# Two fused attention functions: query-first scores issued two slots ahead, and the maxima turned in a step's last slot or inside a projection

## The reference, cut to what matters

```
x = x + _L0_attn_ref(_layernorm(x), ...)    # softmax attention with rotary q, k, and a gated linear-attention recall
x = x + _L0_xattn_ref(ctx_512, ...)         # learned graph, top-k mask
x = x + _L0_ffn_ref(_layernorm(x), ...)     # mixture of experts, 8 choices per token
x = x + _L1_attn_ref(_layernorm(x), ...)    # softmax(q k^T / sqrt(32)) v, then w_o
x = x + _L1_xattn_ref(_layernorm(x), ctx_512, ...)   # the same with keys and values from ctx, causal
x = x + _L1_ffn_ref(_layernorm(x), ...)     # gated network with a Walsh-Hadamard transform
```

## Time and profile before

| what | value |
|---|---|
| measured, median of 3 runs | 3028.73 us |
| the profiled execution: its span | 3028.2 us |
| what lies around the span, by the median | 0.5 us |
| PE busy | 2476.7 us, 82% of the span |
| PEld (weight loads) | 1644.7 us, 54% |
| DVE busy | 1884.0 us, 62% |
| ACT busy | 1239.5 us, 41% |
| POOL busy | 851.9 us, 28% |

### The profile page before, as it was taken

The page is one execution under the profiler, slowest core; times in us unless marked ns, Lnnn a source line. Parts: engine busy times, 40 slices in busy tenths (PEclk is TensorE's granted clock), DMA queues, the critical chain, the costliest instruction groups (busy, mean ns, idle before and its releaser), DMA issues. The chain is left out here.

```text
span 3028.2 us, 35090 instructions
## 1 busy us (share of the span) xinstructions
PE 2476.7 (82%) x12822; PEld 1644.7 (54%) x12822; DVE 1884.0 (62%) x2959; ACT 1239.5 (41%) x1873; POOL 851.9 (28%) x1176
## 2 busy tenths in 40 slices
PE   5898989864443357999448999999999879999999
PEld 4454545321222237998334554545555538888887
DVE  3766575627899985778557777565655444444443
ACT  2444444428656625666103433334333323333332
POOL 2232222215657634555343332001211110000000
PEclk8999999976665678999768999999999979999999
DMA  3213132212222346988585655334433423101000
GB/s 117 65 43 84 43 84 46 70 61 77 77 80 77 108 163 213 308 300 289 158 185 136 159 146 157 88 89 104 109 95 91 115 80 127 42 0 42 1 28 15
DMA packets 186940, 323.55 MB, mean 107 GB/s; under 512 B 20450, under 2 KB 52066, under 8 KB 186788
## 3 DMA queue, kind: packets, MB, share of 16 engines
q1 hardware_dynamic: 168356, 270.44, 30.0%
q0 software_dynamic: 15360, 50.34, 6.3%
q10 hardware_dynamic: 3072, 0.79, 0.1%
HBM read 182.30 MB, written 62.92 MB: 81 GB/s over the span
## 5 line engine op out<-in xcount | busy, mean ns | idle before, releaser
L757 DVE TENSOR_REDUCE at_negmax<-at_ps 128x2 f32<-128x1024 f32 (+3 forms) x256 | 259.1, 1016 | 120.3 <-PE at_ps L523 63.1
L670 ACT ACTIVATE at_probs<-at_ps 128x1024 f32<-128x1024 f32 (+3 forms) x256 | 221.7, 866 | 267.4 <-PE at_ps L538 263.3
L1367 DVE TENSOR_REDUCE a_negmax<-a_ps 128x2 f32<-128x1024 f32 x128 | 155.2, 1217 | 136.4 <-PE a_ps L1120 135.8
L59 PE MATMUL ff_ps<-ff_xnT_hi,ff_s_hi 128*128 128x512 f32 x512 | 200.8, 392 | 5.1 <-DVE ff_xnT_lo L2878 5.1
L60 PE MATMUL ff_ps<-ff_xnT_lo,ff_s_hi 128*128 128x512 f32 x512 | 200.1, 391 | 0.0
L61 PE MATMUL ff_ps<-ff_xnT_hi,ff_s_lo 128*128 128x512 f32 x512 | 200.1, 391 | 0.0
L1946 ACT ACTIVATE gr_act_signs<-gr_signed,gr_test 128x512 bf16<-128x512 f32 x248 | 177.4, 717 | 42.3 <-POOL gr_test L2339 20.4
L2908 DVE TENSOR_TENSOR ff_hid<-ff_hid,ff_ps 128x512 f32<-128x512 f32 x64 | 44.0, 688 | 238.6 <-ACT ff_hid L2853 238.6
L538 PE MATMUL at_ps<-at_qk 98*128 98x512 f32 (+3 forms) x512 | 171.7, 417 | 21.0 <-DMA at_qk<-at_mrow 10.6
L1268 ACT ACTIVATE a_probs<-a_ps 128x1024 f32<-128x1024 f32 x128 | 130.8, 1023 | 135.2 <-PE a_ps L1138 134.6
L518 PE MATMUL at_ps<-at_qk 96*128 96x512 f32 (+3 forms) x512 | 162.9, 382 | 19.0 <-DVE at_xnT_lo L818 8.9
(11 more groups left out here) (431 smaller groups left out, 6640.1 us busy)
## 6 DMA issues: line engine op xcount, KB each, us to landing
at_qk<-at_part SPq DMA_DIRECT2D x384, 128.0 KB
first_gu<-in_L_ffn_w_gate_up_dram SPq DMA_DIRECT2D x32, 1024.0 KB, 13.4
a_qk<-a_part SPq DMA_DIRECT2D x192, 128.0 KB
first_d<-in_L_ffn_w_down_dram SPq DMA_DIRECT2D x32, 512.0 KB, 13.6
out_rows<-ex_y SPq DMA_DIRECT2D x32, 512.0 KB
gr_aside_raw<-in_L_ffn_W_dram SPq DMA_DIRECT2D x48, 256.0 KB, 3.1
w13T<-gr_aside_out SPq DMA_DIRECT2D x32, 256.0 KB, 3.2
shared_x<-x_after_cross SPq DMA_DIRECT2D x8, 1024.0 KB
```

Source lines behind the costliest of these rows:

```text
L59: pe.matmul(out, lh, rh, start=start, stop=False, skip_group_check=True)
L670: act.activation(probs[:, t % 2, 2 * w:2 * w + 2, lo:S], banks(("kq", g, s), lo), ACT.Exp, scale=SCALE).then_inc(free(("kq", g, s)), 1)
L757: dve.reduce_max(negmax[:, g % 2, :].rearrange("p (j t) -> p j t", t=NT)[:, 2 * w:2 * w + 2, t], banks(("qk", g, s), 0, width(g, t)), AX.X ...
L1367: dve.reduce_max(negmax[:, g % 2, :].rearrange("p (j t) -> p j t", t=NT)[:, 2 * w:2 * w + 2, t], banks(("qk", g, s)), AX.X, negate=True).t ...
```

## The change

**Second function.** `score_units(g, s)` puts the query-first unit two slots ahead (LEAD = 2) of its old place: step g issues unit (g+1, s+2) in slot s up to slot 5, and units 0 and 1 of group g+2 in slots 6 and 7. Step -1 does three units in slot 0 to get ahead. The maxima of g+1 are turned in slot 7 (MAXIMA_AT), behind that slot's scores, and the rows are copied and sent there, by the engines' programs too, and no longer at the step's end.

**First function.** In an even step g above 0 the units are two ahead and end with slot 5; slots 6 and 7 have none, and the maxima are turned in slot 7. Step 0 has no lead. In an odd step slots 0 to 5 hold unit s of g+1 as before, slot 6 holds units 6 and 7, and slot 7 units 0 and 1 of g+2. The maxima are then turned inside the first projection, after two of its four contraction chunks for q. The outputs move from the end of step 4k and slots 1, 3, 5 of step 4k+1 to slots 1, 3, 5, 7 of step 4k+1. Weighting and sums stay one half per slot.

The diff, without the repeats of the same edits in ACT's and DVE's programs of the first function:

```diff
@@ -353,6 +353,13 @@
         def reciprocal_part(s):
             return s - 2 if 2 <= s < 2 + NT else None
 
+        LEAD, MAXIMA_AT = 2, PAIRS - 1
+
+        def score_units(g, s):
+            at = PAIRS * (g + 1) + s + LEAD
+            units = range(LEAD + 1) if (g, s) == (-1, 0) else (at,) if g >= -1 else ()
+            return [(n // PAIRS, n % PAIRS) for n in units if has(n // PAIRS)]
+
         SUMS_AT = {1: 0, 6: 1, "mid_end": 2, "end": 3}
 
         def sums_at(g, when):
@@ -365,8 +372,10 @@
             for s in range(PAIRS):
                 if has(g):
                     place("kq", g, s)
-                if has(g + 1):
-                    place("qk", g + 1, s)
+                for unit_of in score_units(g, s):
+                    place("qk", *unit_of)
+                if s == MAXIMA_AT and has(g + 1):
+                    place("mx", g + 1)
                 kind, b, u = unit(g, s)
                 if kind == "o" or kind == "v":
                     place(kind, b, u)
@@ -377,8 +386,6 @@
                     place("xT", b, 1)
                 if weight(g, s) is not None:
                     place("w", weight(g, s))
-            if has(g + 1):
-                place("mx", g + 1)
             if has(g + 3):
                 place("p", g + 3)
 
@@ -637,8 +644,10 @@
                 for s in range(PAIRS):
                     if has(g):
                         scores_kq(g, s)
-                    if has(g + 1):
-                        scores_qk(g + 1, s)
+                    for unit_of in score_units(g, s):
+                        scores_qk(*unit_of)
+                    if s == MAXIMA_AT and has(g + 1):
+                        turn_maxima(g + 1)
                     if s >= 2 and has(g):
                         half(g, s - 2)
                     if s < 2 and has(g - 1):
@@ -654,8 +663,6 @@
                         turn_x(b)
                     if weight(g, s) is not None:
                         turn_weight(weight(g, s))
-                if has(g + 1):
-                    turn_maxima(g + 1)
                 if has(g + 3):
                     project(g + 3)
 
@@ -716,8 +723,8 @@
                             act.copy(xnT[0][:, 2 * i:2 * i + 2, :], banks(("xT", b, i))).then_inc(xT_hi, 1)
                     if weight(g, s) is not None:
                         keep_weight(weight(g, s))
-                if has(g + 1):
-                    maxima_rows(g + 1)
+                    if s == MAXIMA_AT and has(g + 1):
+                        maxima_rows(g + 1)
                 if has(g + 3):
                     if g + 3 >= 1:
                         act.wait_ge(stack_in[(g + 2) % STACKS], 16 * 3 * QUAD * ((g + 2) // STACKS + 1))
@@ -789,8 +796,10 @@
                     dve.wait_ge(masks_made, 2)
                     dve.tensor_copy(above_r, above).then_inc(mask_ready, 1)
                 for s in range(PAIRS):
-                    if has(g + 1):
-                        maxima(g + 1, s)
+                    for unit_of in score_units(g, s):
+                        maxima(*unit_of)
+                    if s == MAXIMA_AT and has(g + 1):
+                        maxima_rows(g + 1)
                     if reciprocal_part(s) is not None and has(g - 1):
                         reciprocals(g - 1, reciprocal_part(s))
                     for b, j in sums_at(g, s):
@@ -955,7 +962,8 @@
         ps = ctx.enter_context(nc.psum_tensor(f"{tag}_ps", [P, 8, 512], F32))
         NUM, SUMS = 6, 7
         STEPS = range(1 - NC, G + 2)
-        OUT_AT = {(0, PAIRS): 0, (1, 1): 1, (1, 3): 2, (1, 5): 3}
+        OUT_AT = {(1, 1): 0, (1, 3): 1, (1, 5): 2, (1, 7): 3}
+        LEAD, MAXIMA_AT = 2, PAIRS - 1
         VALUES_AT = {(2, 0): 0, (2, PAIRS): 1}
 
         def has(g):
@@ -963,6 +971,18 @@
 
         def chunk(g):
             return CHUNKS[g % NC]
+
+        def score_units(g, s):
+            if g % 2 == 0:
+                ahead = LEAD if g > 0 else 0
+                units = [(g + 1, s + ahead)] if s + ahead < PAIRS else []
+            elif s < PAIRS - LEAD or g < 0:
+                units = [(g + 1, s)]
+            elif s == PAIRS - LEAD:
+                units = [(g + 1, s + n) for n in range(LEAD)]
+            else:
+                units = [(g + 2, n) for n in range(LEAD)]
+            return [u for u in units if has(u[0])]
 
         def out_unit(g, s):
             t, b = OUT_AT.get((g % NC, s)), g // NC - 1
@@ -1006,8 +1026,10 @@
             for s in range(PAIRS):
                 if has(g):
                     place("kq", g, s)
-                if has(g + 1):
-                    place("qk", g + 1, s)
+                for unit_of in score_units(g, s):
+                    place("qk", *unit_of)
+                if g % 2 == 0 and s == MAXIMA_AT and has(g + 1):
+                    place("mx", g + 1)
                 if linear_unit(g, s, 2) is not None:
                     place("m", linear_unit(g, s, 2))
                 if linear_unit(g, s, 4) is not None:
@@ -1019,7 +1041,7 @@
                 if turn_unit(g, s) is not None:
                     place("xT", turn_unit(g, s), 0)
                     place("xT", turn_unit(g, s), 1)
-            if has(g + 1):
+            if g % 2 and has(g + 1):
                 place("mx", g + 1)
             if g % 2 and has(g + 3):
                 place("p", g + 3)
@@ -1190,12 +1212,14 @@
                     mm = pe.matmul(bank(key, i), spare(m)[:, 1, i * P:(i + 1) * P], features(m)[:, 0, :], start=True, stop=True, skip_group_check=True)
                 mm.then_inc(l_ready, 1)
 
-            def project(g):
+            def project(g, between=None):
                 at = chunk(g) * P
                 wait_drained(pe, "xT", g // NC, 1)
                 key = claim("p", g)
                 for i, w in enumerate((wqT, wkT)):
                     for dc in range(NC):
+                        if between is not None and (i, dc) == (0, 2):
+                            turn_maxima(between)
                         mm = split_mm(pe, bank(key, i), [p[:, dc, at:at + P] for p in w], [p[:, dc, :] for p in xnT], dc == 0, dc == NC - 1)
                 mm.then_inc(p_ready, 1)
 
@@ -1248,11 +1274,11 @@
                         values(*values_unit(g, s))
                     if turn_unit(g, s) is not None:
                         turn_x(turn_unit(g, s))
-                if has(g + 1):
+                if g % 2 and has(g + 3):
+                    project(g + 3, g + 1 if has(g + 1) else None)
+                    project(g + 4)
+                elif g % 2 and has(g + 1):
                     turn_maxima(g + 1)
-                if g % 2 and has(g + 3):
-                    project(g + 3)
-                    project(g + 4)
                 if out_unit(g, PAIRS):
                     outputs(*out_unit(g, PAIRS))
                 if values_unit(g, PAIRS):
...
```

## The result

The median is 3052.39 us (3048.65 to 3054.88, 4 runs) against 3030.36 for the kernel before in the same measurement: ratio 1.0065, 95% interval 1.0047 to 1.0082, so 14 to 25 us slower. The forecast was 3032, its range ended at 3046. The profiled execution took 3050.13 us with a span of 3048.3, 20.1 over the earlier trace rows.

A forecast was written before the change was run, and what follows sets the result against it. PE's waits were taken to bound the kernel. First function +13.0 us, second -8.5, sum +4.5 on the profiled execution gave 3033.2; 1.2 off for the clock terms gave 3032 us, range 3012 to 3046.

The forecast's parts named there:

- The sum of the second function: Second function: -23.4 us for waits that go, +14.9 us for waits that come, together -8.5 us.
- the late stack: Second function, slot 6 of steps 4 and 8: PE waits 5.0 and 3.8 us for the stack; +14.2 us with clock.
- the low clock: PE runs at granted clock 0.50 after a long wait: 2.7 us added to each wait of over 3 us.
- the removed transposes: Second function, maxima turned at the step's end: 23 waits of PE for the last reduction go, -18.6 us.
- just in time: Second function, step 0: the queue is done with the stack before slot 6 needs it, so no wait was charged.
- covered: Second function, steps with c = 1, 2 and 3: outputs or values before slot 6 cover the stack, no wait charged.
- with the clock at 0.50 behind it: First function, near 310 and 455 us: low clock follows the projection's wait; 5.7 us each with it, +11.4 us.
- What is late next is nothing: Second function, step's end: once the reduction wait goes, no other wait replaces it; the projection hides the rows' copying.
- The knot of outputs, oT, the copy of the recall and the projection's bank: First function, steps 5 and 9: later outputs make PE wait 3.0 to 3.5 us before the projection; +11.4 us with clock.
- the rows of maxima and the stack at step 5: First function, after steps 4, 8, 12: PE idles 3.4 us for rows, then 2.6 for the stack; +5.4 us in all.
- the stack that decides everywhere: Slower rival, chance 0.18: stacks pace steps from their start; landing 1.2 us later costs 12 us in ten causal steps, 3044.
- The term for the DMA of the last rows: Second function, last boundary but one: rows' DMA starts 1.3 us earlier among queued loads; -2 us, bounds 0 to -7.5.

The follow-up runs named there:

- second_only: Only the second attention function has the change, the first is that of the kernel before: 3044.25 us, ratio 1.0037 to before.
- second_load_behind: As second_only, but SyncE issues the 1 MB load of x of steps 0, 4 and 8 behind the stack: 3028.27 us, ratio 0.9990 to before.
- its control: The kernel before with only the load of x issued behind the stack: 3035.98 us beside 3035.11, ratio 0.9995.
- first_only: Only the first attention function has the change, the second is that of the kernel before: 3041.70 us, ratio 1.0037 to before.
- first_outs_early: As first_only, but the four output tiles lie in slots 0, 1, 3, 5 instead of 1, 3, 5, 7: 3035.89 us, ratio 1.0021 to before.

## Why the prediction was wrong

- **The second function's sign: the failed step.** The sum of the second function, -23.4 + 14.9, failed in three of its terms, which the next points take one by one: the late stack was put too low, the low clock was charged only to waits of over 3 us, and the removed transposes were credited in full. Its terms regrouped by the steps above (forecast, measured in the profile; the forecasts come to -8.9, 0.4 off the prediction's own sum by rounding): steps 0, 4, 8: +11.8, +20.1; the steps with g mod 4 = 1: -0.5, +6.2; steps 16, 20, 24: -3.1, +2.5; the other sixteen: -11.7, -9.4; 29 and 30: -4.2, -5.1; the start -1.2, -1.6. So 22 us lie between forecast and measurement, 8 in the late stacks and 12 in steps where PE still waits about as long as before and mostly at a lower clock.
- **The late stack: right cause, too small.** Steps 4 and 8 were forecast with waits of 5.0 and 3.8 us; they are 6.9 and 6.3. I read the end of the transfers from the first microsecond in which the queue's share fell. The queue went on with a few packets (8 in the microsecond from 1744; 17 and 1 in the two from 1865), and the pair waits for the last. Step 0, "just in time", waited 3.16 us (1.26 in second_only), and step 1, "covered", 1.84: a margin of nothing, read from one execution, is no zero. second_load_behind and its control show that the 1 MB ahead in the queue is a cause, worth 14 us once the stack is due early. It is not all of the wait: 3.15 and 3.92 us stayed without it.
- **The clock behind short waits: missed.** I charged the low clock only to waits of over 3 us, because these were the rows that I had looked at. In the profile after, steps 5, 9, 13, 16, 21 and 24 lost 1.5 to 1.7 us of PE time each to it, behind waits of 0.2 to 1.3 us in pairs. Part of this is the luck of one execution: by the counts above the old order loses the clock in 3 of the seven steps with g mod 4 = 1 on average and the new one in 4.3, which at 1.5 us each is an estimate of 2 us and not 6.
- **The clock behind the projection's stall.** At the 2.84 us stalls of the profile after, where I did charge it, it didn't come: 5.4 us too much in the first function, so the sign "with the clock at 0.50 behind it" failed in this execution, and it came behind one of the two in first_only. The 5.4 us were made up by stack waits of 1.95, 0.54 and 1.58 us in steps 3, 7 and 11 (forecast: about 0.5 each, of which 0.2 net) and by the low clock of steps 5 and 9.
- **The transposes: 13 of the 18.6 us.** Seven of those 23 still wait, 0.5 to 1.6 us, 5.5 in sum: three for the bank of a weight that DVE or ScalarE is still splitting, four for a reduction on a DVE that lags, in steps 12, 16, 20 and 24. "What is late next is nothing" was wrong for them. (The six steps with g mod 4 = 1 that the 18.6 leaves out waited 4.0 us in sum in the trace of before, not 4.2.)
- **The first function: right by its steps.** The knot of outputs, oT, the copy of the recall and the projection's bank stalled PE for 2.84 us twice, forecast 3.0 to 3.5, and the rows of maxima and the stack at step 5 took 3.29 and 2.20 us, forecast 3.4 and 2.6 (the 3.4 doesn't follow from its own terms, 3.9 less 1.0; the sum doesn't use it). That the total, 12.4, came so near to 13.0 is in part luck: the errors named under the projection's stall cancel.
- **The rival that came closest** was the stack that decides everywhere, by its size (3044 with a range to 3046), but not by its mechanism: the causal steps 20 and 24 waited 0.55 and 0.43 us, much as in the forecast (0.5 and 0.2), and no other causal step did.
- **The term for the DMA of the last rows** was -2 for step 29. The wait went from 7.48 to 6.70 us, -0.8, and lay between 4.4 and 8.9 in the experiments. The rule of the Trainium skill (DMA: Bandwidth & Descriptors, "Queues, rings and completion order") would have made it about -5; this pair of traces does not bear that out, and the scatter of the experiments leaves it open.

## What to carry to other kernels

Work that is issued earlier needs its operands earlier: before moving it, look at what is queued ahead of each operand's DMA, and move that behind it in the same edit. Short waits have a price beyond their length too, because the clock may fall behind them; whether it does varies from one execution to the next, so count it over several traces before you charge it or explain a step by it. And try the smallest lead that hides the wait; here one slot did no worse than two, and its waits for the stack were shorter.

## What the runs showed of the hardware

- The granted clock can fall to its lower level behind short waits of PE, and whether it does is partly chance. Two waits of 1.02 and 0.48 us, 0.7 us of work apart, were followed in the kernel after by some 3 us at 0.50 (half a sum 1.94 us against 1.06). Two of 1.02 and 0.54 us, 1.7 us of work apart, left the clock at 1.00 in before and were followed by the low clock in first_only. A single wait of 1.25 us ahead of the transpose in step 16 left it up in before and not in first_outs_early, whose second function is that of before (step length 19.9 and 21.4 us).
- Behind the single wait of 2.84 us ahead of the projection's matmuls the clock stayed at full speed in three of four cases (after and first_only, two each). The window from 0.5 us behind the first one in the kernel after:

```profile
307.90:311.00 3.10, 3.10 (x16) 2.41 (x15) 1.75 (x4) 0.00 (x0) 0.00 (x0) 1.00 0.02 5
```

- In the causal steps the same program (step 20) came with a granted clock of 1.00 in one execution (after) and 0.92 in another (second_only), 1.5 us apart, so such a step's length is partly chance.
- A 1 MB load on SyncE's queue ahead of 12 small DMAs delayed the first use of the stack: without it the pair started 5.9 us earlier in step 4 (16.6 us into the step and not 22.5) and 1.9 us earlier in step 8. GpSimd's gathers ran on another queue beside both.
